# First attention of a four-stage kernel: products taken out of PSUM, VectorE's work reordered, GpSimd's gathers split in two groups

## The reference, cut to what matters

```python
qg = split_heads(tokens @ Wqg, 16)              # 16 queries and 64 gates per head
kv = split_heads(tokens @ Wkv, 16)              # 16 keys and 64 values per head
queries, keys, values = l2norm(queries), l2norm(keys), l2norm(values)
attn = jnp.square(jax.nn.relu(einsum('bhid,bhjd->bhij', queries, keys)))
aggr = einsum('bhij,bhjd->bhid', attn, values)
out  = tanh(|aggr|) * aggr / |aggr| * jnp.tanh(jax.nn.silu(gates))
return out @ Wout
```

## Time and profile before

| | |
|---|---|
| timed runs, median | 1835.48 us (1835.18 to 1840.15) |
| profiled execution | 1857.31 us, its span 1854.6 us |
| first attention, about | 380 to 1198 us of the span |
| TensorE busy | 1273.5 us (69%) |
| VectorE busy | 1229.5 us (66%) |
| GpSimd busy | 926.3 us (50%) |
| ScalarE busy | 740.7 us (40%) |
| mean granted TensorE clock | 0.790 |

### The profile page before, as it was taken

The page is one execution under the profiler, slowest core; times in us unless marked ns, Lnnn a source line. Parts: engine busy times, 40 slices in busy tenths (PEclk is TensorE's granted clock), DMA queues, the critical chain, the costliest instruction groups (busy, mean ns, idle before and its releaser), DMA issues.

```text
span 1854.6 us, 27625 instructions
## 1 busy us (share of the span) xinstructions
PE 1273.5 (69%) x8554; PEld 857.2 (46%) x8555; DVE 1229.5 (66%) x2820; ACT 740.7 (40%) x1207; POOL 926.3 (50%) x996
## 2 busy tenths in 40 slices
PE   2434332548888887878788887568778777783775
PEld 1222221425666666656566667523333333331665
DVE  6778771157788887777777784266777677663443
ACT  1101100335455554455445544145555555552322
POOL 2355566546666666666666644321332313223663
PEclk8555555568888888888988886669988898986988
DMA  4000002600000000000000000030000000000110
GB/s 130 25 16 26 14 2 52 132 12 2 7 8 8 7 6 3 3 6 6 6 6 6 7 4 4 16 104 13 18 10 17 9 17 17 9 12 21 60 58 13
DMA packets 73493, 41.41 MB, mean 22 GB/s; under 512 B 23825, under 2 KB 68729, under 8 KB 73424
## 3 DMA queue, kind: packets, MB, share of 16 engines
q1 hardware_dynamic: 53040, 28.88, 5.6%
q0 software_dynamic: 20384, 11.67, 3.1%
HBM read 31.63 MB, written 23.87 MB: 30 GB/s over the span
## 4 chain that ended last, share of the span: by engine, by line
PE 40%; DVE 33%; issue 10%; ACT 6%; POOL 5%; DMA 2%; another core or an unknown queue 1%; POOLq 1%; DVEq 0%; SPq 0%; ACTq 0%
PE psum L1111 8%; PE psum L1162 5%; PE psum L1216 4%; DVE terms L1731 4%; DVE o L1573 4%; PE psum L1345 2%; PE psum L1358 2%; POOL o_inv L634 2%; PE psum L1139 2%; PE psum L1239 2%; PE psum L1249 2%; PE psum L1277 2%; PE psum L1120 1%; DVE rden L1425 1%; POOL xe_dram L573 1%
## 5 line engine op out<-in xcount | busy, mean ns | idle before, releaser
L1111 PE MATMUL psum<-v,attn 128*128 128x64 f32 x2048 | 288.5, 301 | 25.7 <-ACT aggr L845 17.1
L1111 PEld LDWEIGHTS psum<-v,attn 128*128 128x128 f32 x2048 | 272.7, 214 | 61.6 <-issue 44.9
L1731 DVE TENSOR_REDUCE terms<-psum 128x2 bf16<-128x512 f32 x256 | 165.5, 690 | 37.2 <-PE psum L1239 28.5
L609 POOL DMA_INDIRECT yg<-ye_dram,routel x128 | 139.2, 1088 | 65.5 <-issue 36.0
L695 POOL TENSOR_SCALAR veps<-meanvar 128x2 f32<-128x2 f32 x32 | 6.1, 191 | 330.9 <-DVE meanvar L1709 329.8
L573 POOL DMA_INDIRECT xe_dram<-rows_out,route x128 | 131.1, 1024 | 39.6 <-issue 38.7
L1216 PE MATMUL psum<-prob,v 128*32 128x256 f32 x1024 | 148.8, 415 | 1.1 <-ACT pvT L919 0.8
L914 ACT ACTIVATE prob<-psum 128x512 f32<-128x512 f32 x256 | 138.5, 597 | 18.8 <-PE psum L1204 18.8
L830 ACT ACTIVATE attn<-psum 128x1024 f32<-128x1024 f32 x128 | 129.9, 1015 | 11.9 <-PE psum L1094 10.7
L1120 PE MATMUL psum<-ident,o 128*128 128x128 f32 x256 | 48.5, 351 | 102.3 <-DVE o L1573 78.9
L1239 PE MATMUL psum<-k_highT,q_highT 32*128 32x256 bf16 x512 | 56.6, 303 | 76.9 <-DVE terms L1731 73.0
(11 more groups left out here) (297 smaller groups left out, 2975.8 us busy)
## 6 DMA issues: line engine op xcount, KB each, us to landing
x4n_dram<-x4n SPq DMA_DIRECT2D x16, 256.0 KB
w<-in_w POOLq DMA_DIRECT2D x48, 64.0 KB, 2.5
x_in<-in_x SPq DMA_DIRECT2D x8, 256.0 KB, 2.8
xe_dram<-zero_rows SPq DMA_DIRECT2D x8, 256.0 KB, 3.5
x_dram<-x1s SPq DMA_DIRECT2D x8, 256.0 KB
xe_dram<-rows_out,route POOLq DMA_INDIRECT x128
xe<-xe_dram SPq DMA_DIRECT2D x16, 128.0 KB
x1l<-x_dram SPq DMA_DIRECT2D x16, 128.0 KB, 2.2
```

The costliest lines, as they stand in the source:

```text
L609: pool.indirect_dma_start(yg[p][:, j, k, :], None, ye_dram, bass.IndirectOffsetOnAxis(ap=where[:, j, K0 + k:K0 + k + 1], axis=0), bounds_c ...
L1111: mm = pe.matmul(psum[:, 4 + j, (head % HALF) * DV:(head % HALF + 1) * DV], attn[g % RING][:, h, c * SEQ + j * P:c * SEQ + (j + 1) * P], v ...
L1731: dve.tensor_reduce(terms4[:, 0, j, head:head + 2, 6, 0], bank[4 + a2].rearrange("q (b k) -> q b k", b=2), AX, ALU.max, negate=True).then_ ...
```

## The change

Four things, all in the first attention:

1. **Products out of PSUM.** VectorE's square becomes relu times score, with the score read from PSUM, for six pairs (0, 1, 3, 5, 6, 7); pairs 2 and 4 are squared by ScalarE; GpSimd squares nothing. TensorE's next scores into the same banks wait for that product, not for the relu. `aggr` and its copy are gone: VectorE multiplies the aggregate in PSUM by the unscaled gate (`product_with_gate`, two of 512 columns), while ScalarE squares the other bank (each bank is read by one engine at a time). `o` has two buffers.
2. **The factor comes last.** GpSimd scales `o` in place (`scale_output`) instead of the gate.
3. **VectorE reordered.** `product_with_gate(tail, 1)` at g = 1, before the copies of the values; `norm_of(tail, 1)` from g = 1 to g = 2, behind `take_oT(tail, 0)`, the values' copies and `x2_kept`; `combine` in two parts, at g = 4 and g = 6; `normalise3` from g = 6 to g = 7, behind the last copy of keys; `take_oT(tail, 1)` and `norm_of(att, 0)` before `split_terms`.
4. **GpSimd reordered.** Four gathers, the length and the scaling of `tail`'s half 1, four gathers, the values, the reciprocal deviation, and then the length and scaling of `att`'s half 0 (its length stood before the deviation).

```diff
-            def gather_slots(p):
+            def gather_slots(p, part):
                 for j in range(2):
-                    for k in range(K0):
+                    for k in range(2 * part, 2 * part + 2):
                         pool.indirect_dma_start(
 ...
-                        ).then_inc(s["yg_landed"][p], 16)
+                        ).then_inc(s["rest_landed" if part else "yg_landed"][p], 16)
-            def scale_gate(q, hf):
-                hold(s["gate_made"], 2 * q.n)
+            def scale_output(q, hf):
                 hold(s["o_tanh_made"], 2 * (q.n - 1) + hf + 1)
 ...
+                hold(s["o_product"], 4 * (q.n - 1) + 2 * hf + 2)
                 for j in range(2):
-                    part = gate[q.p][:, j, 512 * hf:512 * hf + 512].rearrange("q (h d) -> q h d", d=DV)
+                    part = o[hf][:, j, :].rearrange("q (h d) -> q h d", d=DV)
 ...
-                    ins.then_inc(s["gated"], 1)
+                    ins.then_inc(s["o_made"], 1)
             def half(fetch, front, att, tail):          # GpSimd
-                        gather_slots(fetch.p)
+                        gather_slots(fetch.p, 0)
                 if tail:
                     length_of(tail, 1)
-                if att:
-                    square(att, POOL_PAIRS[0])
-                if tail:
-                    scale_gate(tail, 1)
-                if att:
-                    square(att, POOL_PAIRS[1])
+                    scale_output(tail, 1)
+                if fetch and (not isinstance(fetch.n, int) or fetch.n > 1):
+                    gather_slots(fetch.p, 1)
                 if front:
 ...                                                     # values times inverse norms
-                if att:
-                    length_of(att, 0)
                 if fetch:
 ...                                                     # reciprocal deviation
                 if att:
-                    scale_gate(att, 0)
-                if att:
-                    square(att, POOL_PAIRS[2])
+                    length_of(att, 0)
+                    scale_output(att, 0)
             def take_aggregate(q, hf):                  # ScalarE
-                act.activation(aggr[:], psum[:, 4:6, :], ACT.Copy).then_inc(s["aggr_out"], 1)
-                act.activation(aggr_sq[:], aggr[:], ACT.Square).then_inc(s["aggr_sq_made"], 1)
+                act.activation(aggr_sq[:, 0, :], psum[:, 4, :], ACT.Square).then_inc(s["aggr_sq_made"], 1)
+                act.wait_ge(s["o_product"], 4 * (q.n - 1) + 2 * hf + 1)
+                act.activation(aggr_sq[:, 1, :], psum[:, 5, :], ACT.Square).then_inc(s["aggr_sq_made"], 1)
             def half(fetch, front, att, tail):          # ScalarE
+                    if att and g in ACT_PAIRS:          # behind the values' squares (g = 2) or the gates (g = 4)
+                        square(att, g)
+                    if front and g == 4:
+                        gate_tanh(front, 0)
             def scores(att, g):                         # TensorE
-                wait(pe, s["relu_made"], PAIRS * (att.n - 1) + g - 1)
+                before, n = (g - 2) % PAIRS, att.n - 1 - (g < 2)
+                if before in ACT_PAIRS:
+                    wait(pe, s["relu_made"], PAIRS * n + before + 1)
+                else:
+                    wait(pe, s["attn_made"], len(DVE_PAIRS) * n + DVE_PAIRS.index(before) + 1)
             def square(q, g):                           # VectorE
-                dve.tensor_tensor(r[:], r[:], r[:], ALU.mult).then_inc(s["attn_made"], 1)
+                dve.tensor_tensor(r[:], r[:], psum[:, 2 * (g % 2):2 * (g % 2) + 2, :], ALU.mult).then_inc(s["attn_made"], 1)
-            def gated_output(q, hf):
-                dve.wait_ge(s["gated"], 4 * (q.n - 1) + 2 * hf + 2)
-                dve.tensor_tensor(o[:], aggr[:], gate[q.p][:, :, 512 * hf:512 * hf + 512], ALU.mult).then_inc(s["o_made"], 1)
+            def product_with_gate(q, hf):
+                dve.wait_ge(s["gate_made"], 2 * q.n)
+                dve.wait_ge(s["attn_read"], PAIRS * (q.n - 1) + 4 * hf + 4)
+                for j in (1, 0):
+                    if j == 0:
+                        dve.wait_ge(s["aggr_sq_made"], 4 * (q.n - 1) + 2 * hf + 1)
+                    dve.tensor_tensor(o[hf][:, j, :], psum[:, 4 + j, :], gate[q.p][:, j, 512 * hf:512 * hf + 512], ALU.mult).then_inc(s["o_product"], 1)
             def half(fetch, front, att, tail):          # VectorE
+                    if tail and g == 1:
+                        product_with_gate(tail, 1)
 ...                                                     # g 1, 2: sums of squares, copies of the values
-                    if att and g == 1:
+                    if att and g == 2:
 ...                                                     # x2_kept
+                        take_oT(tail, 0)
+                    if tail and g == 2:
                         norm_of(tail, 1)
-                    if tail and g == 1:
-                        take_oT(tail, 0)
-                    if tail and g == 4:
-                        gated_output(tail, 1)
+                    if fetch and g == 4:
+                        combine(fetch, 0)
+                    if att and g == 5:
+                        product_with_gate(att, 0)
+                        norm_of(att, 0)
+                    if tail and g == 5:
+                        take_oT(tail, 1)
                     if front and g == 5:
                         split_terms(front)
-                    if fetch and g == 5:
-                        combine(fetch)
+                    if fetch and g == 6:
+                        combine(fetch, 1)
 ...                                                     # x3 (g 6), copies of keys (g 6, 7)
-                    if fetch and g == 6:
+                    if fetch and g == 7:
                         normalise3(fetch)
-                    if att and g == 7:
-                        gated_output(att, 0)
```

More of the change, by code:

```diff
@@ L250, in build_program @@
         s = {}
-        for name in ("scattered", "w_landed", "w2_landed", "x1l_landed", "routel_landed", "yg_landed"):
+        for name in ("scattered", "w_landed", "w2_landed", "x1l_landed", "routel_landed", "yg_landed", "rest_landed"):
             s[name] = sems(name)
@@ L262, in build_program @@
             s[name] = sem(name)
-        early = [x for name, value in s.items() if name not in ("scattered", "w_landed", "w2_landed", "x1l_landed", "routel_landed", "yg_landed", "yg_cleared", "cleared")
+        early = [x for name, value in s.items() if name not in ("scattered", "w_landed", "w2_landed", "x1l_landed", "routel_landed", "yg_landed", "rest_landed", "yg_cleared", "cleared")
                  for x in (value if isinstance(value, list) else [value])]
@@ L316, in build_program @@
         attn = [sb(f"attn{n}", [P, 2, 512]) for n in range(RING)]
-        aggr = sb("aggr", [P, 2, 512])
         aggr_sq = sb("aggr_sq", [P, 2, 512])
-        o = sb("o", [P, 2, 512])
+        o = two("o", [P, 2, 512])
         oT = sb("oT", [P, 2, PAIRS, P])
@@ L336, in build_program @@
         G_BANK = ((1, 0), (1, 0))
-        POOL_PAIRS = (2, 3, 6)
+        ACT_PAIRS = (2, 4)
+        DVE_PAIRS = tuple(g for g in range(PAIRS) if g not in ACT_PAIRS)
         scope.pop().close()
@@ L830, in relu, with square @@
                 act.activation(r[:], psum[:, 2 * (g % 2):2 * (g % 2) + 2, :], ACT.Relu).then_inc(s["relu_made"], 1)
+            def square(att, g):
+                act.wait_ge(s["relu_made"], PAIRS * (att.n - 1) + g + 1)
+                r = attn[g % RING]
+                act.activation(r[:], r[:], ACT.Square).then_inc(s["attn_made_act"], 1)
             def square_of(front, k, src):
@@ L837, in gate_tanh @@
             def gate_tanh(front, j):
-                wait(act, s["o_made"], 2 * (front.n - 2))
+                wait(act, s["o_product"], 4 * (front.n - 2))
                 act.wait_ge(s["silu_made"], 4 * (front.n - 1) + 2 * j + 2)
@@ L887, in half @@
                         take_oT(tail, 1)
-                    if front and g == 5:
-                        gate_tanh(front, 0)
                     if att and g == 5:
@@ L1099, in aggregate @@
                 if g % 4 == 0:
-                    wait(pe, s["aggr_out"], 2 * (q.n - 1) + hf)
+                    wait(pe, s["aggr_sq_made"], 4 * (q.n - 1) + 2 * hf)
+                    wait(pe, s["o_product"], 4 * (q.n - 1) + 2 * hf)
                 if g == 0:
                     pe.wait_ge(s["v_made"], q.n)
-                if g in POOL_PAIRS:
-                    pe.wait_ge(s["attn_made_pool"], len(POOL_PAIRS) * (q.n - 1) + POOL_PAIRS.index(g) + 1)
+                if g in ACT_PAIRS:
+                    pe.wait_ge(s["attn_made_act"], len(ACT_PAIRS) * (q.n - 1) + ACT_PAIRS.index(g) + 1)
                 else:
-                    pe.wait_ge(s["attn_made"], (PAIRS - len(POOL_PAIRS)) * (q.n - 1) + g - sum(x < g for x in POOL_PAIRS) + 1)
```

(26 more changed lines are left out.)

22 lines of the change are left out of this document (9 added, 13 removed).

## The result

The changed kernel takes **1949.77 us** (median of 4 runs, 1943.09 to 1951.16) against 1837.82 us before (4 runs, 1835.18 to 1840.95) on the same chip: ratio 1.0601, 95% interval 1.0569 to 1.0634. Forecast were 1899 us and a range up to 1941. The direction was right, the size was not: 112 us more, not 64.

A forecast was written before the change was run, and what follows sets the result against it. No engine alone but a loop from turn to turn was taken as the bound. Turns of 54.3 instead of 48.68 us give 67 us over twelve, last three -2, first turns 0: 65, scaled to 64, so 1899 us; range 1856 to 1941.

The forecast's parts named there:

- The loop: Dependency closing from turn to turn, cut at four events into A, B, C and D; 47.97 us before the change.
- A: From tail's last aggregate's end to the end of norm_of(tail, 1): 4.16 us before, 11.5 forecast.
- B: From the end of norm_of(tail, 1) to the start of that length's tanh: 4.92 us before, 3.9 forecast.
- C: From that tanh to the end of fetch's mean and variance: 23.91 us before, forecast 21.9, or 23.1 with slow TensorE.
- D: From fetch's mean and variance to the next turn's last aggregate: 14.98 us before, forecast 15.2, or 17.4 with slow TensorE.
- The first gap: TensorE idle about 4 us before pair 2's aggregate, waiting for ScalarE's square; taken as near enough to lower its clock.
- the second: TensorE idle 2 to 3 us before the second group of terms; taken as not lowering its clock.
- 48.68 on average: Base turn before the change, from twelve turns between the first and thirteenth x3, 584.15 us in one profile.
- about 4 each: Saving in the last two turns, without front, from losing the wait for the scaled gate and a copy.
- PSUM products held: Rival: GpSimd still holds VectorE's PSUM products; 2.5 us a turn more, 1930 us; chance 0.06.
- The clock stays up: Rival: gap before pair 2 stays short enough; 51 to 52.5 us a turn, about 1865 us; chance 0.16.
- The shorter turn: Rival: removed stops decide, TensorE and VectorE run through; 45 us a turn, 1783 us; chance 0.12.

The follow-up runs named there:

- experiment 2: The changed kernel with norm_of(tail, 1) back in step 1, directly behind its product; 1898.78 us, ratio 1.0325 to the kernel before.
- experiment 3: The changed kernel with GpSimd's length of half 0 ahead of the layer norm's power again; 1914.05 us, ratio 1.0415.
- experiment 4: The changed kernel with both orders restored, the norm of tail's half 1 early and GpSimd's length of half 0 first; 1826.26 us, ratio 0.9951.
- experiment 9: experiment 5 with GpSimd's length of half 0 put back behind the layer norm's power; 1823.82 us, ratio 0.9954.
- experiment 5: experiment 4 with product and norm of half 1 behind the two value copies, still ahead of take_oT(tail, 0); 1790.08 us, ratio 0.975.
- experiment 10: experiment 5 with all eight gathers together at the start of GpSimd's turn; 1763.31 us, ratio 0.963.
- experiment 6: The changed kernel with TensorE's two gate products of step 4 ahead of pair 2's aggregate; 1929.21 us, ratio 1.053.
- experiment 11: experiment 5 with TensorE's gate products of step 4 ahead of pair 2's aggregate; 1788.99 us, ratio 0.9766.
- experiment 8: The kernel before with only VectorE's five squares changed to rectified score times score in PSUM; 1832.48 us, ratio 0.999.
- experiment 7: The changed kernel with all eight gathers at the start of GpSimd's turn, as before the change; 1933.42 us, ratio 1.0545.

## Why the prediction was right in direction and wrong in size

**The loop and its legs: right.** In the turn from 661.41 the last aggregate of the tail ends at 677.26, the norm at 688.67, the tanh starts at 692.48, mean and variance end at 714.42: A 11.4 (forecast 11.5), B 3.8 (3.9), C 21.9 (21.9 at full clock), D, the rest of 54.84, is 17.7 (17.4 with a slow TensorE). Everything that was to show it does. Experiments 2, 3, 4 and 9 confirm A and D as the causes, by undoing them.

**First failed step: "The first gap is near the one that took the clock down (5.4 us), the second is not, so I take 54.3."** The second took it down too (2.85 us, then an aggregate of 3.67). That alone did little harm: 54.3 was taken half-way between 52.5 and 55.9, and the short turns are 54.3 to 54.8. That it fits them is partly luck. TensorE was slow in both places, for which the forecast had 23.1 in C and 17.4 in D; D took 17.7, but C only 21.9, as at full clock. The larger part is a third gap, which the sum had inside leg A and did not consider for the clock. It takes the clock down in six of the twelve turns. It is the wait of the turned output for the value copies:

```profile
568.69 1.09 PE L1121 MATMUL psum<-ident,o 128*128 128x128 f32 x8 [2.14 <-DVE v L1659]
...
570.04 3.31 PE L1112 MATMUL psum<-v,attn 128*128 128x64 f32 x16
573.13 3.73 PE L1149 MATMUL psum<-w_v,x3T 128*128 128x512 f32 x4
```

At full clock they are 2.00 and 1.94. The norm waits for the last copy of these products, so A is 14.1 there (564.78 to 578.91), the rest is nearly as above (B 3.8, C 22.2, D 18.0), and the turn is 58.1. So leg A, forecast at 11.5 for every turn, is 14.1 to 14.3 in half of them: 6 x 2.8 = 17 us. (The distances of the x3 do not match this turn by turn, as the loop is cut elsewhere: one turn of 58 us is without it, one of 54.7 has it.) With the rest, the mean is 56.31 and not 54.3: 12 x 2.0 = 24 us.

**Second: the base.** "48.68 on average" should have been 47.87: 10 us. The single profile of before was 19.5 us longer than the median that it was to stand for; I scaled the difference by 0.988 and so carried the three disturbed turns on as if they were the kernel's own. The list of its turns (47.4 to 48.4 and three of 50.5 to 51.1) gave the hint.

**Third: the ends.** The last two turns, without `front`, were to lose "about 4 each": they took 40.1 and 24.0, before 39.9 and 27.2, so 3 in place of 8; and the turn ahead of them was one of 58, 10.4 more and not 6. Together +7.4 and not -2. "The first turns have nothing of the loop: 0" was wrong as well: the first x3 stands behind a whole tail, and came 7.1 later.

24 + 10 + 9 + 7 - 3 (rest) = 47 of the 48 that were missing.

**Fourth: "That GpSimd has four gathers ahead of it and not eight is worth nothing".** For leg B that was right, the length starts when the norm is there. But the second four stand ahead of the values, which hold the first combine; leg C's GpSimd strand had them in its sum, and I did not weigh leaving them out. Price 16 us on the changed kernel by the medians (13 of them where it can be located in the profile), some 22 on experiment 5 by the ratios.

**The rivals.** *PSUM products held*: fell, 1.21 and 0.69 us beside GpSimd all along (groups L1564 and L1578). *The clock stays up*: fell, its condition (a short gap before pair 2) was not met. *The shorter turn*: it can be had, but not on the condition that was given, a norm at most 6.9 us behind the last aggregate. In experiments 2 and 4 the norm ends 2.7 us behind it and the turns are 53.22 and 47.80; in experiment 5 it ends 5.3 us behind it in the turns of 48.9 and of 43.3 alike. The short ones are under the 45 that the rival gave, and no run with a late norm has any; but an early norm is not enough.

**What stays open.** What decides in which turns the clock falls. The same wait of 2.14 us before the same instruction is followed by an aggregate of 2.00 in one turn (681.17) and of 3.31 in another (568.69). Before the turned output, the waits of 1.19 us of experiments 5 and 10 are followed by an aggregate of 2.00 every time, those of 2.1 us by a slow one in six of thirteen turns of the changed kernel and in twelve of thirteen of experiment 3, those of 3.4 us in nearly all of experiments 2 and 4. So a shorter wait is safer at this place, and its length alone does not decide. That the clock is a cause of the lost time, and not only beside it, is argued from these rows: no experiment changed the clock and nothing else, and the two that were to fill a gap (6 and 11) did not isolate it.

## What to carry to other kernels

Before moving an instruction out of a stop, cut the loop at its events and ask what each leg costs in the new order: here both removed stops were real, and two pieces of work put a few places later, VectorE's norm and GpSimd's length, made a longer loop. Count each gap of the bottleneck engine twice, once as time and once for what the clock makes of the work behind it, and look at every gap of the new order, the small ones too. Take the base from the turns of a profile, not from its span, and leave out turns that differ from their neighbours when the medians say that the profile was a long one.

## What was not expected of the hardware

- In several kernels the turns keep to a few lengths: 47.8 us (before, experiments 4 and 8), 54.5 and 58.1 (the change, experiment 7), 43.3 and 48.9 (experiment 5). In others they scatter, 52.8 to 59.5 in experiment 6 and 43.9 to 51.9 in experiment 9. A microsecond won in a turn that has a stretch at half clock was lost to a longer stretch (experiment 8), and two edits of 51 and 36 us brought 123 together (experiment 4).
- Waits of 2.1 to 3.4 us, with TensorE at full clock before them, are followed by aggregates at half clock (3.31 to 3.67 us, full 2.00), and the clock falls soon behind one of 1.7 us (experiment 5) and one of 1.3 (experiment 11). None that short was in the reckoning; the earlier trace rows had shown 5.4. Not every wait in front of a slow aggregate is the cause: at 699.31 and 648.87 the clock was already down.
- The same kernel in the same order alternates between turns at clock 0.79 and 0.96, 48.9 and 43.3 us (experiment 5).
